# Splitting the head and down weights in another order, and two projections ahead of a down product, in a fused attention and gated-FFN kernel

## What is computed

```python
xn = _layernorm(x, axis=-1)
s = _L0_attn_ref(xn, Wq, bq, Wk, bk, Wv, bv)
g = _silu(_L0_ffn_ref(xn, ln_w, gate_w, up_w, down_w))
x = x + s * g

# attention of a row
q = einsum('bse,edh->bsdh', x, Wq) + bq          # k and v alike, 8 heads, each repeated 4 times
scores = einsum('bsdh,bseh->bsde', q, k) / sqrt(D)
out = einsum('bsde,bseh->bsdh', softmax(scores), v)

# FFN of a row
nx = x * rsqrt(mean(square(x)) + 1e-5) * ln_w
out = (silu(nx @ gate_w.T) * (nx @ up_w.T)) @ down_w.T
```

## Time and profile before

| | us |
|---|---|
| median of 3 runs | 473.84 (473.63 to 474.03) |
| profiled execution | 474.23 |
| its span (first to last instruction) | 472.4 |
| PE busy | 465.8 (99%) |
| DVE busy | 411.9 (87%) |
| ACT busy | 243.7 (52%) |
| POOL busy | 120.7 (26%) |

### The profile page before, as it was taken

One profiled execution on the slowest core, in us unless ns is written; L12 is line 12 of the kernel. 1 busy time (PEld: TensorE's weight loads), 2 busy tenths in 40 slices (PEclk: granted clock), 3 DMA queues, 4 the chain that ended last, 5 costly groups with the idle time before them and its releaser, 6 DMA issues.

```text
span 472.4 us, 6230 instructions
## 1 busy us (share of the span) xinstructions
PE 465.8 (99%) x2130; PEld 391.6 (83%) x2130; DVE 411.9 (87%) x559; ACT 243.7 (52%) x417; POOL 120.7 (26%) x104
## 2 busy tenths in 40 slices
PE   8999999999999999999999999999999999999997
PEld 7899888888888878888888888888888888888886
DVE  6999778987898997989989898999998888888994
ACT  4784665568588888654112545225225335358102
POOL 2920213116221122233443101000011111127920
PEclk9999999999999999999999999999999999999999
DMA  8606997579779996573474649546656655514772
GB/s 269 253 2 239 356 370 263 224 263 259 213 246 307 291 369 248 188 268 133 135 231 167 218 188 366 207 182 223 222 201 223 223 200 201 200 44 135 288 247 89
DMA packets 44623, 105.70 MB, mean 224 GB/s; under 512 B 20272, under 2 KB 21808, under 8 KB 41264
## 3 DMA queue, kind: packets, MB, share of 16 engines
q1 hardware_dynamic: 44592, 105.31, 63.5%
HBM read 69.90 MB, written 35.40 MB: 223 GB/s over the span
## 4 chain that ended last, share of the span: by engine, by line
PE 95%; POOL 2%; DVE 1%; DMA 1%; ACT 0%; issue 0%; SPq 0%; POOLq 0%; DVEq 0%
PE gu_ps L558 18%; PE gu_ps L560 18%; PE gu_ps L561 18%; PE y_ps L700 8%; PE y_ps L701 8%; PE y_ps L702 8%; PE gu_ps L702 3%; PE gu_ps L700 3%; PE gu_ps L701 3%; PE gu_ps L729 2%; PE gu_ps L728 2%; PE gu_ps L733 2%; DMA xz<-x 1%; POOL h_kept L514 0%; PE y_ps L742 0%; PE gu_ps L579 0%
## 5 line engine op out<-in xcount | busy, mean ns | idle before, releaser
L558 PE MATMUL gu_ps<-z_hi,w_ops 128*128 128x512 f32 x378 | 147.2, 389 | 0.0
L560 PE MATMUL gu_ps<-z_lo,w_ops 128*128 128x512 f32 x378 | 147.1, 389 | 0.0
L561 PE MATMUL gu_ps<-z_hi,w_ops 128*128 128x512 f32 x378 | 147.1, 389 | 0.0
L501 POOL TENSOR_TENSOR h_lo<-h,h_hi 128x512 fp32r<-128x512 f32 x28 | 36.8, 1315 | 229.3 <-ACT h_hi L930 229.2
L558 PEld LDWEIGHTS gu_ps<-z_hi,w_ops 128*128 128x128 f32 x378 | 70.9, 188 | 15.2 <-ACT u L905 0.5
L561 PEld LDWEIGHTS gu_ps<-z_hi,w_ops 128*128 128x128 f32 x378 | 71.0, 188 | 14.8
L560 PEld LDWEIGHTS gu_ps<-z_lo,w_ops 128*128 128x128 f32 x378 | 70.9, 188 | 14.6
L700 PE MATMUL y_ps<-wd_ops,h_hi 128*128 128x512 f32 x168 | 65.6, 390 | 0.0
L701 PE MATMUL y_ps<-wd_ops,h_hi 128*128 128x512 f32 x168 | 65.5, 390 | 0.0
L702 PE MATMUL y_ps<-wd_ops,h_lo 128*128 128x512 f32 x168 | 65.5, 390 | 0.0
L930 ACT ACTIVATE h_hi<-h 128x512 fp32r<-128x512 f32 x28 | 17.6, 630 | 58.8 <-DVE h L1229 58.7
(11 more groups left out here) (143 smaller groups left out, 750.1 us busy)
## 6 DMA issues: line engine op xcount, KB each, us to landing
w_kept<-w_ops SPq DMA_DIRECT2D x13, 1792.0 KB, 6.4
w_ops<-w_kept SPq DMA_DIRECT2D x13, 1792.0 KB, 7.6
wd_ops<-wd_kept SPq DMA_DIRECT2D x35, 512.0 KB, 4.2
raw<-gate_up SPq DMA_DIRECT2D x30, 256.0 KB, 4.3
wd_kept<-wd_ops SPq DMA_DIRECT2D x14, 512.0 KB, 7.5
xz<-x SPq DMA_DIRECT2D x16, 256.0 KB, 6.0
raw<-down SPq DMA_DIRECT2D x14, 256.0 KB, 7.8
w_ops<-wd_kept SPq DMA_DIRECT2D x7, 512.0 KB, 7.0
```

What stands on the lines that cost most here:

```text
L501: pool.tensor_tensor(lo, src, hi.bitcast(F32), ALU.subtract).then_inc(h_lo_done, 1)
L558: pe.matmul(acc, w_h, z_hi[:, zi, c, :], start=start and c == 0, stop=False, skip_group_check=True)
L560: pe.matmul(acc, w_h, z_lo[:, zi, c, :], start=False, stop=False, skip_group_check=True)
L561: end = pe.matmul(acc, w_l, z_hi[:, zi, c, :], start=False, stop=c == 1, skip_group_check=True)
```

## The change

Seven moves, nothing added or removed. Line numbers of the changed kernel are one higher from L529 on.

1. SP: `load_down(0)` ahead of the loads of slice 1.
2. GpSimd: the scale and shift of tile 5 ahead of the two bias sums, not behind.
3. PE: projection 1 ahead of the transposition of tile 4, and projection 2 ahead of that of tile 6.
4. PE: projections 8 and 9, not 8 alone, ahead of `down_product(13)`.
5. ACT: `hi_wd(0)` ahead of tile 4's high part, tile 5's high part ahead of `z_tile(7)`.
6. ACT, blocks 1 to 13: `hi_wd(g)` behind `take_u3` (and behind `hi_s` where that comes last) instead of ahead of `take_u2`.
7. DVE: in the start-up tile 6's low part behind `times_up0(0)` and the take of projection 2, and the take of projection 3 ahead of the first `t_add`.

```diff
@@ sync
             load_x(0, (JJ - 1,))
+            load_down(0)
             load_gate(1)
             load_up(1)
-            load_down(0)
             load_down(1)
@@ gpsimd
             scale_tile(J)
+            scale_tile(J + 1)
             pool.wait_ge(bias_in, 48)
...
-            for j in range(J + 1, JJ):
-                scale_tile(j)
+            scale_tile(J + 2)
+            scale_tile(J + 3)
@@ tensor
             qkv_product(0)
+            qkv_product(1)
             second_tile(J)
-            qkv_product(1)
             second_tile(J + 1)
+            qkv_product(2)
             second_tile(J + 2)
-            qkv_product(2)
             second_tile(J + 3)
             qkv_product(3)
...
             qkv_product(JJ)
+            qkv_product(JJ + 1)
             down_product(NI - 1)
-            qkv_product(JJ + 1)
             qkv_product(JJ + 2)
@@ scalar
             z_tile(J + 1)
+            hi_wd(0)
             z_hi_tile(J)
             z_tile(J + 2)
+            z_hi_tile(J + 1)
             z_tile(J + 3)
             z_raw_tile(J)
-            z_hi_tile(J + 1)
             z_hi_tile(J + 2)
-            hi_wd(0)
...
                 hi_a(g + 1)
-                hi_wd(g)
                 take_u2(g)
                 silu0(g)
...
                 take_u3(g)
                 if g <= 2:
                     hi_s(g + 1)
+                hi_wd(g)
                 if g + 2 <= NI:
                     scale(g + 2)
@@ vector
             z_lo_tile(J + 1)
-            z_lo_tile(J + 2)
             times_up0(0)
             qkv_take(2)
+            z_lo_tile(J + 2)
             z_lo_tile(J + 3)
+            qkv_take(3)
             t_add(0, 0)
-            qkv_take(3)
```

## The result

The changed kernel takes 474.62 us (median of 17 runs, 474.0 to 475.6); before, measured beside it, 473.76 (17 runs). The ratio is 1.0015, 95% interval 1.0009 to 1.0021: 0.4 to 1.0 us slower; the two medians lie 0.86 apart. The profiled execution took 474.62 with a span of 472.8 us; the one before 474.23 with 472.4.

A forecast was written before the change was run, and what follows sets the result against it. PE, busy 99% of the span in one unbroken stream, was taken as the bound. The terms summed to +1.13 us, 474.23 to 475.36 for the profiled execution, 0.39 above the median: forecast 475.0, range 472.7 to 475.7.

The forecast's parts named there:

- m6 of block 12: End of block 11: L507 holds up DVE's dense stretch, so PE's m6 load in block 12 comes late, +1.05 us.
- the 0.28 at m7: Block 11: with hi_wd(11) behind take_u3 its DMA has landed, so PE's m7 doesn't wait, -0.28 us.
- Start-up, -0.64: Start-up: projection 1 fills PE's hole ahead of tile 4's transposition; first gate product at 26.97, not 27.61 us.
- the foretold wait of 0.36: Start-up: the third projection waits for DVE's take of projection 0 and starts at 21.76, 0.36 us lost.
- the three ways: End of block 11: L507 waits for L1271, then holds lo_s 0.75 us; or costs 1.09; or goes first, costing 1.34.
- Projection 8, +0.90: End of block 13: L507 falls among lo_s and two z2_lo on DVE, delaying the projection that reads them, +0.90 us.
- The down product, -0.26: End of the pass: two projections side by side give h_lo(13) 2.1 us more, removing the 0.26 hole before the down product.
- the third projection, +0.36: End of the pass: its qkv_take on DVE comes 1.3 us later behind held-up z2_lo, so PE waits, +0.36 us.
- Blocks 2, 3, 6, 0 to +0.3: Ends of 2 and 3, and 6: c12 or ACT's seeds at most 0.4 us late; put at nothing, range 0 to +0.3.
- rival (c): SyncE: in block 6 L507 delays lo_s(7), then keep_w(7) and SP's queue up to m6(11); 475.6 us, chance 0.10.
- (a): Ends of blocks 11 and 13: neither hold reaches PE, the gains alone count, -1.18, 472.7 us; chance 0.20.
- (b): Only one hold lands: block 11's gives 473.7 us, the end of the pass 473.9; chance 0.25.

The follow-up runs named there:

- e1: Kernel before with only the start-up's moves (1, 2, 3, 5 and 7); 473.38 us against 473.93, ratio 0.9989.
- e2: Kernel before with only move 4, projections 8 and 9 side by side ahead of the last down product; ratio 1.0003.
- e3: Kernel before with only move 6, hi_wd(g) behind take_u3 in blocks 1 to 13; ratio 1.0036.
- e4: Changed kernel with two GpSimd waits: low part of down slice 11 behind lo_s(12), of slice 13 behind the second z2_lo; ratio to before 0.9990.
- e5: Changed kernel with GpSimd's L507 subtraction of slice 13 done twice into the same place; ratio to before 1.0043.
- e6: Changed kernel with hi_wd(g) between take_u2 and silu0 in blocks 1 to 13, instead of behind take_u3; ratio to before 0.9980.

## Why the prediction came out

The time, 474.62, lies 0.4 under the forecast of 475.0 and the direction is as forecast, slower, though by 0.15% and not by over 0.2%: by the prediction's own bound (474.79) it is one of the cases called the same. The mechanism was right and two terms were mis-sized, in opposite directions: m6 of block 12 cost 0.70 less than forecast, and the 0.28 at m7 is nothing for most executions. That they partly cancel is luck.

- **Start-up, -0.64:** -0.61 in the profile, with the third projection at 21.74 (21.76) and the low part of tile 7 ended at 26.84 (26.83). PE's own part of the working is off by 0.4 (tile 4's transposition at 20.92, not 20.53), which the foretold wait of 0.36 took in. The close agreement is in part luck, as the start alone varies by more than the term between executions; the 0.5 of e1 is what the move is worth. e1 shows a gain in the median, and in its own profile that some of it can be given back in block 11.
- **m7 of block 11, -0.28:** right for the profiled execution, wrong for the median. The step that failed is the costing of a wait for a DMA from one execution: the hole is in one of four executions with this code (before, its two repetitions, e2).
- **m6 of block 12, +1.05:** this step failed. It measured 0.35. Of the three ways the one with 0.75 of hold happened, and I took the middle one by the earlier trace rows. That way came to 0.51 and not 0.75: a whole hold costs DVE 1.09 to 1.11 and not the 1.30 of L507's record, and c22 fills 0.60 of it; the forecast 0.75 is about what the full 1.30 would leave. The seed ended 1.14 behind c12 (178.42 against 177.28), not 1.25, probably as silu1 followed an ACT operation without a pause. The Trainium skill's rule ("SBUF — State Buffer", section "SBUF: two separate sides"), that the one that starts first has the pair for the whole instruction, decides this case rightly: L1272 at 171.48, L507 at 171.59 and done at 173.86. By that rule the term would have been 0.7, which takes away half the error. It doesn't hold for every operation of GpSimd: z_scale, in the last section, started first and held nothing up.
- **Projection 8, +0.90:** 0.83 in all three executions, in e3 0.84, with L507 0.04 to 0.05 ahead of lo_s each time; shown to be the hold and not ACT's order by e4 (gone), e5 (1.09 more for one more hold) and e6.
- **The down product, -0.26, and the third projection, +0.36:** -0.26 and +0.30.
- **Blocks 2, 3, 6, 0 to +0.3:** no hole. In block 6 lo_s(7) was held up (2.19 us) but DVE's idle time took it in. The condition of rival (c) was met: on the clock of the trace before lo_s(7) ended at 113.29, behind 113.0, and keep_w(7) was issued at 113.46, 0.41 later than 113.05. What didn't follow is the rest: at the loads of slice 12 the lag was down to 0.14 (issued at 154.84, before at 155.31), and m6 of block 11 has no hole.

With the measured terms the profile's sum is -0.61 - 0.28 + 0.35 + 0.83 - 0.26 + 0.30 = +0.33, and the profiled executions differ by 0.39. Without the -0.28, which most executions don't have to lose, it is +0.61, or +0.7 with e1's 0.5 for the start-up; the timed ratio says +0.71. A second count goes round the start-up: from the first gate product to the last matmul's start the kernel before takes 440.73 and 440.75 in its repetitions, the changed one 442.18 to 442.23 in all three executions, 1.36 more once the 0.11 of the start-up is off. The holes give 1.22 of it; the other 0.14 stands in no hole listed here. Rivals (a) and (b) are out: both holds reach PE, each time.

## What to carry to other kernels

When a helper operation of GpSimd is moved, look at what VectorE does where it now lands: beside a reduction or a transposition, or in a wait, it cost nothing here, in a dense stretch of two-input operations up to 1.1 us of DVE's time for an operation of 1.3, and PE felt it where that stretch feeds it. A wait for a DMA that one profile shows is a term with a chance, not a term; a second profile of the same kernel tells. And before moving something to the far side of a wait, try the near side: one place further up, behind take_u2, had none of the holes (e6).

## What was not expected of the hardware

The record of a blocked GpSimd operation starts when it is ready, not when it runs: L507 has 1.29 to 1.30 us free and 2.27 behind DVE's product. GpSimd's busy time rose from 120.7 to 123.7 us with the same work, 1.1 of it in the L507 records. When both engines had an operation waiting, the one that was ready first ran first, and each GpSimd operation cost DVE 1.1 us (e5). Not every operation of GpSimd holds DVE up: z_scale of 128x8 (L544, 1.64 us) had been running for 0.37 us when lo_s(7) started in the kernel before, and lo_s took its usual 1.21. In the other order z_scale does wait: behind the held lo_s(7) of the changed kernel its record is 2.62. And landings differ by over a microsecond between executions: the down slice of block 11 took 11.37 us from issue to landing in one profile of the changed kernel and 9.89 in another, while the up weights of slice 12 kept within 3.54 and 3.94 but for the 4.42 of e1.
